# Last key's values through the output weights as products of their own, two comparisons on GpSimd, and the last three slots in another order

## What is computed

```python
x = x + xattn(layernorm(x), ctx)      # 16 heads, 257 keys of 192 features per batch
x = x + local(layernorm(x))           # each token sees 2 neighbours on either side
x = x + ffn(layernorm(x))             # 8 experts, one per token

def xattn(x, context):
    q, k, v = x @ Wq, context @ Wk, context @ Wv      # split by head
    attn = softmax(q @ k.T * scale)
    return (attn @ v) @ Wo

def ffn(x):
    e = argmax(x @ Wr + br)
    h = gelu(x @ W1[e] + b1[e])       # 256 -> 1024
    h = gelu(h @ W2[e] + b2[e])       # 1024 -> 512
    return h @ W3[e] + b3[e]          # 512 -> 256
```

## Time and profile before

| | us |
|---|---|
| median of 3 runs | 708.28 |
| the 3 runs | 708.06, 708.28, 709.68 |
| the profiled execution | 709.04 |
| its span | 707.2 |

### The profile page before, as it was taken

The page is one execution under the profiler, slowest core; times in us unless marked ns, Lnnn a source line. Parts: engine busy times, 40 slices in busy tenths (PEclk is TensorE's granted clock), DMA queues, the critical chain, the costliest instruction groups (busy, mean ns, idle before and its releaser), DMA issues.

```text
span 707.2 us, 26666 instructions
## 1 busy us (share of the span) xinstructions
PE 687.9 (97%) x9301; PEld 581.3 (82%) x9302; DVE 475.2 (67%) x1462; ACT 451.4 (64%) x1073; POOL 442.9 (63%) x595
## 2 busy tenths in 40 slices
PE   8999999999999999999999969999999999999996
PEld 7888888888888888888888857888888888888885
DVE  4467777777777777777788889999943990278000
ACT  4656666666666676666666653666675757575753
POOL 6476665656566565656565635676767786777643
PEclk9999999999999999999999989999999999999998
DMA  7433233333323333343357324248034431262000
GB/s 214 119 87 85 70 78 96 93 82 82 96 72 93 94 88 74 76 96 91 87 154 246 129 83 165 97 123 300 23 106 159 170 113 60 82 223 65 25 7 1
DMA packets 56178, 74.35 MB, mean 105 GB/s; under 512 B 6589, under 2 KB 41950, under 8 KB 56128
## 3 DMA queue, kind: packets, MB, share of 16 engines
q1 hardware_dynamic: 49792, 60.63, 30.4%
q0 software_dynamic: 2992, 8.26, 3.8%
q10 hardware_dynamic: 3344, 4.80, 1.9%
HBM read 67.30 MB, written 7.27 MB: 105 GB/s over the span
## 4 chain that ended last, share of the span: by engine, by line
PE 92%; DVE 2%; issue 1%; ACT 1%; DMA 1%; POOL 1%; ACTq 0%; POOLq 0%; SPq 0%; DVEq 0%
PE ps_s L2023 18%; PE ps_kv L1603 12%; PE ps_kv L1611 11%; PE ps_p L1689 8%; PE ps_o L1675 6%; PE ps_s L1622 6%; PE ps_p L1971 4%; PE ps_kv L1971 4%; PE ps_o L2037 4%; PE ps_s L2002 2%; PE ps_m L1808 2%; PE ps_m L1754 2%; PE ps_m L1727 2%; PE ps_m L1812 2%; PE ps_s L2031 1%
## 5 line engine op out<-in xcount | busy, mean ns | idle before, releaser
L868 ACT ACTIVATE prob<-prob,neg_max 128x257 f32<-128x257 f32 x256 | 111.2, 501 | 42.9 <-DVE neg_max L1105 41.2
L1105 DVE CUSTOM_DVE_ANT_0 prob<-ps_s,mask_add 128x257 f32<-128x257 f32 x256 | 94.7, 421 | 64.0 <-PE ps_s L1622 63.7
L1573 DVE CAST w<-w_raw 128x512 fp32r<-128x512 f32 x94 | 71.0, 756 | 56.3 <-DMA w_raw<-in_L_ffn_W_dram 56.3
L1576 DVE TENSOR_TENSOR w<-w_raw,w 128x512 fp32r<-128x512 f32 x112 | 101.6, 910 | 3.7
L681 POOL TENSOR_TENSOR ctx_parts<-ctx_raw,ctx_parts 128x512 fp32r<-128x512 f32 x64 | 83.1, 1299 | 23.5 <-ACT ctx_parts L863 21.6
L2023 PE MATMUL ps_s<-w,h_hi 128*128 x368 | 91.1, 399 | 0.7 <-ACT h_hi L1017 0.6
L1611 PE MATMUL ps_kv<-wkv_hi,ctx_parts 128*128 128x256 f32 x512 | 84.6, 293 | 0.1
L1603 PE MATMUL ps_kv<-ctx_parts,wkv_hi 128*128 128x256 f32 x512 | 84.2, 292 | 0.2 <-POOL ctx_parts L681 0.2
L694 POOL COPY last_prob<-prob 128x4 f32<-128x4 f32 x64 | 12.1, 189 | 113.1 <-ACT prob L868 109.0
L876 ACT COPY v<-ps_kv 128x512 f32<-128x512 f32 x64 | 37.5, 587 | 70.2 <-PE ps_kv L1611 70.2
L806 POOL TENSOR_TENSOR h_lo<-h,h_hi 128x512 fp32r<-128x512 f32 x46 | 66.8, 1453 | 24.7 <-ACT h_hi L1004 19.8
(11 more groups left out here) (303 smaller groups left out, 1515.5 us busy)
## 6 DMA issues: line engine op xcount, KB each, us to landing
w_raw<-in_L_ffn_W_dram SPq DMA_DIRECT2D x24, 1024.0 KB, 7.1
ctx_raw<-in_ctx_turned_dram SPq DMA_DIRECT2D x63, 256.0 KB, 3.4
mask_add<-mask_dram SPq DMA_DIRECT2D x64, 128.5 KB, 3.3
w_raw<-in_L_ffn_W_dram SPq DMA_DIRECT2D x8, 512.0 KB, 3.6
rows_dram<-x3n ACTq DMA_DIRECT2D x15, 256.0 KB, 4.2
xt<-in_x_dram SPq DMA_DIRECT2D x16, 128.0 KB, 2.1
xr<-in_x_dram SPq DMA_DIRECT2D x16, 128.0 KB, 2.2
slot_x<-rows_dram,slot_ids POOLq DMA_INDIRECT x23, 3.9
```

Of the source, the lines that this page charges most:

```text
L868: a.activation(prob[:, g, :], prob[:, g, :], ACT.Exp, bias=neg_max[:, g:g + 1], scale=-1.0).then_inc(exp_done, 1)
L1105: d.tensor_tensor_reduce(prob[:, r, :], ps_s[r][:, 0:J], mask_add[:, k, :], -(HD ** -0.5), 3.0e38, ALU.add, ALU.min, neg_max[:, r:r + 1]). ...
L1573: d.tensor_copy(w[:, b, HI, part], raw[:, b, part]).then_inc(rounded, 1)
L1576: last = d.tensor_tensor(w[:, b, LO, part], raw[:, b, part], f32(w[:, b, HI, part]), ALU.subtract)
```

## The change

- The weighted values are kept in attn by half of the features first and batch second, so that the transpose gives attn_turned in the layout of attnT. In the tiles before the last, transpose and add stay as they are.
- For the last tile the add is gone. ScalarE spreads the last key's values into attnT beforehand, in the last tile's third batch. TensorE multiplies these by wo first, then runs 6 fillers in place of 10, waits for the transpose, and adds the product of attn_turned into the same PSUM rows.
- The comparisons of tiles 3 and 4 go from VectorE to GpSimd, behind the shifted band. TensorE adds up their products later, behind the turning of the biases.
- In slot 20 layer 3 is postponed on TensorE; it comes in slot 21, behind six of the eight transposes of z1 of slot 22 and ahead of the turning of z2 of 21. ScalarE does the first layer of 21 ahead of the second of 20. GpSimd makes the LO parts in the order h1 of 21, h2 of 20, h1 of 22, then scatters slot 20, makes h2 of 21, and scatters 21 and 22.
- The output rows of slots 20 and 21 are added up by VectorE from PSUM. In slot 22 ScalarE makes all four activations first and rounds the second pair; VectorE rounds the first pair.

```diff
--- before.py
+++ after.py
@@ -154,8 +154,8 @@
...
         probT = over("probT", "area", place1(2, HI) + 8 * JM, [P, 2, GROUPS * P])
-        attn = sb("attn", [P, BT, GROUPS * HD])
-        attn_turned = passing("attn_turned", [P, BT, 2, S])
+        attn = sb("attn", [P, 2, BT, S])
+        attn_turned = passing("attn_turned", [P, 2, P])

@@ -301,6 +301,7 @@
...
         h2_hi_done = sem("h2_hi_done")
+        last_h2_rounded = sem("last_h2_rounded")
         h2_done = sem("h2_done")
@@ -363,6 +364,7 @@
...
         band_done = sem("band_done")
+        last_vT_spread = sem("last_vT_spread")
         xn1_done = sem("xn1_done")
@@ -457,6 +459,9 @@
...

+        def last_but_two(i):
+            return follows(i, 2) and not follows(i, 3)
+
         def before_by(n, i, run, q):
@@ -471,7 +476,7 @@
...
         MAPPED, ROUTED = 8, 14
-        BY_DVE, BY_POOL = (0, 1, 2, 3, 12, 13, 4, 5, 14, 15), (6, 7, 8, 9, 10, 11)
+        BY_DVE, BY_POOL = (0, 1, 2, 12, 13, 5, 14, 15), (6, 7, 8, 9, 10, 11, 3, 4)
         CHOSEN, STEPS = 4, 7
@@ -773,6 +778,9 @@
...

+            for t in BY_POOL[6:8]:
+                match(t)
+
             last_row = pool.alloc_register("last_row")
@@ -834,7 +842,7 @@
...

-            for i in range(SLOTS):
+            for i in range(SLOTS - 2):
                 if i > 0:
@@ -843,12 +851,14 @@
...
                     lo_xT(i + 2)
-                if not last_but_one(i) and i != LAST:
+                if not last_but_two(i):
                     lo_h2(i)
-                if i + 1 < SLOTS:
-                    lo_h1(i + 1)
-                if last_but_one(i):
-                    lo_h2(i)
+                lo_h1(i + 1)
+            lo_h2(LAST - 2)
+            lo_h1(LAST)
+            scatter_slot(LAST - 2)
+            lo_h2(LAST - 1)
+            scatter_slot(LAST - 1)
             scatter_slot(LAST)
@@ -943,6 +953,10 @@
...
                         copy_probT(n)
+                    if isinstance(T, int) and (T, k) == (TILES - 1, 2):
+                        act.wait_ge(m_filled, turn(T, 3) + 1)
+                        a.copy(attnT[:, :, :].rearrange("p c (b s) -> p c b s", b=BT),
+                               last_vT[:, :, BT * T:BT * (T + 1)].unsqueeze(3).to_broadcast([P, 2, BT, S])).then_inc(last_vT_spread, 1)

@@ -1026,8 +1040,8 @@
...
                     last.then_inc(gelu2_done, 1)
-                    act.wait_ge(gelu2_done, LAST + pair + 1)
-                    a.copy(h2_parts[HI][:, 2 * pair:2 * pair + 2, :], h2[:, 2 * pair:2 * pair + 2, :]).then_inc(h2_hi_done, 1)
+                act.wait_ge(gelu2_done, LAST + 2)
+                a.copy(h2_parts[HI][:, 2:4, :], h2[:, 2:4, :]).then_inc(h2_hi_done, 1)

@@ -1057,13 +1071,17 @@
...
                     second_layer_last(expert_of(i))
-                    copy_y(i - 1, q - 1)
                     return
...
                     second_layer(i, expert_of(i))
+                    return
+                if last_but_two(i):
+                    first_layer(i + 1, expert_of(i + 1))
+                    second_layer(i, expert_of(i))
+                    copy_z1(i + 2)
                     return
@@ -1232,8 +1250,8 @@
...
                     dve.wait_ge(attn_turned_done, T)
-                d.tensor_tensor(attn[:, k, :].rearrange("p (g e) -> p g e", e=HD), weighed[:, :, 0:HD],
-                                row_inv[:, :].unsqueeze(2).to_broadcast([P, GROUPS, HD]), ALU.mult).then_inc(o_done, 1)
+                d.tensor_tensor(attn[:, :, k, :].rearrange("p c (g e) -> p c g e", e=HD), weighed[:, :, 0:HD].rearrange("p (c g) e -> p c g e", c=2),
+                                row_inv[:, :].rearrange("p (c g) -> p c g", c=2).unsqueeze(3).to_broadcast([P, 2, GROUPS // 2, HD]), ALU.mult).then_inc(o_done, 1)

@@ -1332,11 +1350,12 @@
...
                     dve.wait_ge(o_done, BT * T)
-                    d.transpose(attn_turned[:, :, :, :].rearrange("p b c s -> p (b c s)"),
-                                attn[:, :, :].rearrange("p b d -> p (b d)")).then_inc(attn_turned_done, 1)
+                    d.transpose(flat3(attn_turned[:, :, :]), attn[:, :, :, :].rearrange("p c b s -> p (c b s)")).then_inc(attn_turned_done, 1)
+                    if isinstance(T, int) and T == TILES:
+                        return
                     dve.wait_ge(attn_turned_done, T)
                     d.tensor_tensor(attnT[:, :, :].rearrange("p c (b s) -> p c b s", b=BT),
-                                    attn_turned[:, :, :, :].rearrange("p b c s -> p c b s"),
+                                    attn_turned[:, :, :].rearrange("p c (b s) -> p c b s", b=BT),
                                     last_vT[:, :, bass.ds(BT * (T - 1), BT)].unsqueeze(3).to_broadcast([P, 2, BT, S]),
@@ -1454,7 +1473,6 @@
...
                 number_single(1)
-                match(3)

@@ -1478,7 +1496,6 @@
...
                 match_single(1)
-                match(4)
                 dve.wait_ge(tail_filled, filled("values"))
@@ -1581,9 +1598,18 @@
...

-            dve.wait_ge(y_filled, LAST)
-            for pair in range(2):
-                dve.wait_ge(h2_hi_done, LAST + pair + 1)
+            def output_rows(i):
+                q = i % AHEAD
+                dve.wait_ge(slot_in[q], 16 * (i // AHEAD + 1))
+                dve.wait_ge(y_filled, i + 1)
+                d.tensor_tensor(y[:, q, :], ps_y[:, 0:D], slot_x[:, q, 0:D], ALU.add).then_inc(y_done, 1)
+
+            output_rows(LAST - 2)
+            output_rows(LAST - 1)
+            dve.wait_ge(gelu2_done, LAST + 1)
+            d.tensor_copy(h2_parts[HI][:, 0:2, :], h2[:, 0:2, :]).then_inc(last_h2_rounded, 1)
+            for pair, hi_done in enumerate((last_h2_rounded, h2_hi_done)):
+                dve.wait_ge(hi_done, LAST + 1 if pair else 1)
                 d.tensor_tensor(h2_parts[LO][:, 2 * pair:2 * pair + 2, :], h2[:, 2 * pair:2 * pair + 2, :],
@@ -1902,16 +1928,19 @@
...
                 rank_single(1, ps_p[:, 0:E]).then_inc(ranked, 1)
-                keep_clock(10)
                 my_turn(TILES, 0)
-                pe.wait_ge(attnT_done, TILES)
+                pe.wait_ge(last_vT_spread, 1)
                 for c in range(2):
-                    last = t.matmul(ps_m[:, 0:D], attnT[:, c, :], wo[:, c, :], start=(c == 0), stop=(c == 1))
+                    t.matmul(ps_m[:, 0:D], attnT[:, c, :], wo[:, c, :], start=(c == 0), stop=False)
+                keep_clock(6)
+                pe.wait_ge(attn_turned_done, TILES)
+                for c in range(2):
+                    last = t.matmul(ps_m[:, 0:D], attn_turned[:, c, :], wo[:, c, :], start=False, stop=(c == 1))
                 last.then_inc(tail_filled, 1)
...
                 t.matmul(ps_kv[:, P:P + D + E], turned0[:, 2 * P:3 * P], lv[:, 0:D + E], start=True, stop=True).then_inc(tail_filled, 1)
-                fill_chunks(0, 1, 2, 3, 6, 7, 8, 9)
+                fill_chunks(0, 1, 2, 6, 7, 8, 9)
                 keep_clock(14)
@@ -1926,7 +1955,7 @@
...
                 last.then_inc(tail_filled, 1)
-                fill_chunks(13, 4)
+                fill_chunks(13)
                 keep_clock(2)
@@ -1939,7 +1968,7 @@
...
                 keep_clock(5)
-                fill_chunks(14)
+                fill_chunks(3, 4, 14)
                 rank_single(3, ps_m[:, E:2 * E])
@@ -2041,7 +2070,10 @@
...
                 pe.wait_ge(h2_hi_done, i + 1)
-                pe.wait_ge(y_copied, i)
+                if last_but_one(i):
+                    pe.wait_ge(y_done, i)
+                else:
+                    pe.wait_ge(y_copied, i)
                 t.matmul(ps_y[:, 0:D], ones_r[:, :], b3_parts[:, bass.ds(e * D, D)], start=True, stop=False)
@@ -2057,8 +2089,8 @@
...
                 pe.wait_ge(w23_ready, 3 * e + 3)
-                for pair in range(2):
-                    pe.wait_ge(h2_hi_done, LAST + pair + 1)
+                for pair, hi_done in enumerate((last_h2_rounded, h2_hi_done)):
+                    pe.wait_ge(hi_done, LAST + 1 if pair else 1)
                     layer3_products(e, PRODUCTS[0:2], range(2 * pair, 2 * pair + 2), ps_last)
@@ -2101,12 +2133,14 @@
...
                     turn_z1_pair(i + 1, 1, 0)
+                if last_but_one(i):
+                    layer3(i - 1, postponed.pop())
                 turn_z2(i)
...
                     layer1(i + 2, ahead)
-                if last_but_one(i):
+                if last_but_two(i) or last_but_one(i):
                     postponed.append(expert)
```

## The result

| | before | after |
|---|---|---|
| median of 6 runs, us | 708.31 (707.43 to 709.68) | 705.83 (704.89 to 706.63) |
| profiled execution: own time, span, us | 709.04, 707.2 | 706.63, 704.9 |

The ratio of the times is 0.9966, with a 95% interval of 0.9955 to 0.9976: 2.5 us faster, where 2.45 was forecast and a median of 705.8.

What follows compares the result with a forecast made beforehand. TensorE, busy 97% of the span, was taken as the bound, with waits in the last attention tile and last expert slots. Terms 0.4 - 0.15 + 1.3 + 0.3 + 0.6 = 2.45 us gave median 705.8, range 704.9 to 707.1.

Steps and rivals of the forecast that it cites:

- The first product: Last attention tile: last key's values multiplied separately, so the add goes; 0.4 us gained, bounds 0.1 and 0.6.
- rival (e): More than forecast: the first product gains its 0.6 and nothing is lost, 705.2 us; chance 0.10.
- GpSimd's comparisons: Last tile: two comparisons moved to GpSimd slow VectorE's exposed steps; 0.15 us lost, bounds 0 and 1.2.
- Rival (a): Last tile: GpSimd's four instructions hold VectorE's exposed steps, 1.2 us lost and not 0.15, 706.9; chance 0.13.
- The order of the slots: Last three slots: slot 20's third layer moves into TensorE's 1.41 us gap; 1.3 us gained, bounds 0 and 1.4.
- 0.1 for that: Slot 22's second layer: 0.1 us allowed for its fourth rounded pair, ready near 690.9 when TensorE comes to its matmuls.
- The shared rounding: Slot 22: VectorE rounds the first pair beside ScalarE, last rounding sooner; 0.3 us gained, bounds 0 and 0.4.
- The last scatter: Kernel's end: slot 21's rows done sooner, so the last scatter follows its sum; 0.6 us gained, bounds 0.4 and 0.7.
- Rival (b): GpSimd's queue at the end: slot 21's low part over 0.5 us late, 0.5 to 1 us given back; chance 0.14.
- Rival (c): Last slots: reordering does not fill the gap, slot 22's activations still bound it, 1.3 us missing, 707.1; chance 0.03.
- Rival (d): TensorE's clock returns to full after the slots' start, each us at half clock costing 0.5; 710.5 or more, chance 0.04.
- What would show it: Signs named: product near 407.0, masking 0.2 to 0.4 earlier, no TensorE wait over 0.2, last scatter 0.3 after its sum.

Runs made afterwards that it cites:

- products_undone: changed_again with VectorE's add of the last key's values and ten fillers back, ScalarE's spread copy out; 705.82 us, ratio 0.9964.
- pair_early: changed_again with the last two z1 transposes of slot 22 put ahead of slot 20's third layer; 705.7 us, ratio 0.9957.
- changed_again: The changed kernel with one line more, TensorE reading each slot's expert number within stated bounds; 705.66 us, ratio 0.9959 to the kernel before.
- round_act: changed_again with ScalarE rounding both pairs of the last slot and VectorE none; 705.62 us, ratio 0.9957.
- rows_old: changed_again with output rows of slots 20 and 21 through ScalarE's copy and GpSimd's add again; 706.28 us, ratio 0.997.
- tail_only: The kernel before with only the changes of the attention stage and last tile, last slots as before; 707.51 us, ratio 0.9988.
- no_fillers: changed_again without the six fillers between the last tile's two output products; 705.59 us, ratio 0.9951.

## Why the prediction was right

**The first product, 0.4 forecast, 0.41 measured** (products_undone), with 0.07 where 0.04 stood for the residual add. The working held in its parts. With the 0.94 us by which the scaling came later taken off, the second product started at 406.96 (near 407.0) and ended at 407.99 (408.06). The choice between the bounds was right for the reason given, that TensorE was itself busy: with the fillers out, *add* is 1.93, 0.71 less than before, which is rival (e)'s 0.6 and the 0.07. (That rival's 705.2 doesn't follow from its two terms, which give 0.35 more than forecast, 705.5.) The spread copy fitted, and the changed layout cost nothing: from the transpose of tile 0 to that of tile 13 the trace has 318.73 us in both profiles, before and after.

**GpSimd's comparisons, 0.15 lost forecast, none measured.** This term was mis-sized, within its bounds. Single steps do grow, by 0.02 to 0.04 us, but where they did the path had slack: the masking waited for TensorE (0.16 us at 415.89). GpSimd's part came out as worked: done at 417.09 less the shift, for 417.1, and a slack of 1.40, for 1.5 (its rows, 414.77 and twice 0.61 + 0.81, give 417.6 before the shift and not 417.5, and with that the slack is 1.4). Rival (a), 1.2 lost, is out: *mask* is 9.08 with the comparisons on either engine.

**The order of the slots, 1.3 forecast, 1.14 measured.** The place of each step was right: the last second layer started at 688.37, which with the 0.20 us by which slot 20's copy came earlier is 688.57, for 688.56. What was mis-sized is the "0.1 for that", the fourth pair's lateness: 0.29, shown by pair_early, which takes it out. I had put the third pair's wait for the late transposes into it, but as a wait of about 0.1, and it came through whole.

**The shared rounding, 0.3 forecast, 0.32 to 0.39 measured** (0.36 after, 0.32 in changed_again, 0.39 back in round_act). VectorE's rounding took 0.28, not the 0.4 that I had feared doubled.

**The last scatter, 0.6 forecast, 0.61 measured.** 0.46 of it is VectorE's sums (rows_old). The other 0.15 comes by subtraction: 1.31 before, 1.16 with the old rows in the new order. In tail_only it is 1.24.

**Rival (b)**, GpSimd late with slot 21's low part, was priced on too narrow a margin: the low part ended at 694.45 and TensorE's low products started at 695.49, 1.04 us and not 0.5. **Rival (c)** is out by the chain: the gap is filled. **Rival (d)**, the clock, was nearer than its row told. In the kernel after the clock fell between 421.25 and 421.75, and came back between 428.25 and 428.75, just before slot 0's work; in changed_again it came at 429.5 and in no_fillers at 429.25, and slot 0's transposes ran at half clock in the one and began at it in the other. So a sign that was named for being wrong did come, half clock after the first slot's start, but it cost 0.74 and 0.44 us of *first slot*, not the 2.45 that the rival needed.

**What would show it** held otherwise: no TensorE wait over 0.2 us in the chain from 680 to 695 but the one named, the last scatter 0.28 after its sum, the end of the last second layer 1.14 earlier to that of slot 20. The masking was 0.47 earlier by the distance, more than the 0.2 to 0.4 named.

The sum of the terms as measured is 0.48 + 1.14 + 0.36 + 0.61 = 2.59 us. The forecast 2.45 is close to it partly because two errors of size cancel: 0.15 too much taken off for contention, 0.16 too much given to the order.

## What to carry to other kernels

Price a change by the stretch between two landmarks that enclose it, not by clock times or whole spans: here edits of 0.2 to 0.5 us came back within 0.04 us in distances, while medians of the same kernels could not be told apart. Where a wait is filled with moved work, go on to the next thing that work delays: the third layer filled 1.41 us and held back two small transposes, which cost 0.29. And filler that keeps an engine busy is itself work in a queue: where it stands between an operand's arrival and its use it can cost more than it holds.
